# Split operands for two more experts' second products, and the first two gated experts run by halves

## The reference, cut to what matters

```python
logits = tokens @ router_w.T
topv, topi = jax.lax.top_k(logits, K)                 # K = 2 of E = 8
w = jax.nn.softmax(topv, axis=-1)
gate = zeros((T, n_experts)).at[arange(T)[:, None], topi].add(w)
for e in range(n_experts):
    h = gelu(tokens @ w1[e].T)                        # 128 -> 256
    y = h @ w2[e].T                                   # 256 -> 128
    out = out + gate[:, e:e + 1] * y
```

## Time and profile before

| | |
|---|---|
| median of 3 runs | 139.96 us (139.6 to 140.53) |
| the profiled execution, its own time | 139.31 us |
| its span, first to last instruction | 137.6 us |
| mean granted TensorE clock | 0.937 |
| busy: TensorE, VectorE, ScalarE, GpSimd | 83%, 83%, 60%, 28% |

### The profile page before, as it was taken

One profiled execution on the slowest core, in us unless ns is written; L12 is line 12 of the kernel. 1 busy time (PEld: TensorE's weight loads), 2 busy tenths in 40 slices (PEclk: granted clock), 3 DMA queues, 4 the chain that ended last, 5 costly groups with the idle time before them and its releaser, 6 DMA issues.

```text
span 137.6 us, 1963 instructions
## 1 busy us (share of the span) xinstructions
PE 113.8 (83%) x598; PEld 82.6 (60%) x598; DVE 113.6 (83%) x324; ACT 82.4 (60%) x157; POOL 38.3 (28%) x59
## 2 busy tenths in 40 slices
PE   6999999999999999999999998885999200068990
PEld 4686768477565788877664877763768100045670
DVE  5898985998419999999947897889698899799872
ACT  3542495825756658787436124177978999860730
POOL 1018302230359910069301284422021011100000
PEclk9999999999999999999999999999999955555999
DMA  4995000000159722222000000000000000000004
GB/s 122 369 412 231 0 0 0 0 0 22 64 156 341 261 74 91 75 78 76 0 5 0 0 0 2 5 0 2 0 0 0 0 2 0 0 0 0 5 0 152
DMA packets 4413, 8.76 MB, mean 64 GB/s; under 512 B 417, under 2 KB 1825, under 8 KB 4146
## 3 DMA queue, kind: packets, MB, share of 16 engines
q1 hardware_dynamic: 4400, 8.62, 17.8%
q10 hardware_dynamic: 2, 0.00, 0.0%
HBM read 8.07 MB, written 0.56 MB: 63 GB/s over the span
## 4 chain that ended last, share of the span: by engine, by line
PE 59%; DVE 20%; issue 9%; ACT 5%; POOL 4%; DVEq 0%; POOLq 0%
PE bank L1441 7%; PE bank L1392 6%; PE bank L1387 6%; PE bank L1389 5%; PE bank L1421 5%; PE bank L1269 4%; PE bank L1295 3%; PE bank L1290 3%; PE bank L1289 3%; DVE amax_p L1164 3%; POOL q_soft L487 2%; PE bank L1624 2%; DVE amax_g L1155 2%; PE bank L1275 2%; DVE hidden L1200 2%
## 5 line engine op out<-in xcount | busy, mean ns | idle before, releaser
L1269 PE MATMUL bank<-zero 128*128 128x256 f16 x112 | 18.7, 321 | 15.7 <-ACT ng L706 14.0
L567 ACT ACTIVATE hidden<-bank 128x512 f32<-128x512 f32 x32 | 18.6, 593 | 12.4 <-PE bank L1392 11.2
L1269 PEld LDWEIGHTS bank<-zero 128*128 128x128 f16 x112 | 12.4, 114 | 19.6 <-ACT ng L706 14.5
L1387 PE MATMUL bank<-xhi,we_hi 128*128 128x512 f32 x32 | 17.2, 538 | 0.0
L993 DVE TENSOR_TENSOR hidden<-hidden,q_exp 128x512 f32<-128x512 f32 x12 | 10.2, 873 | 4.7 <-DMA q_exp<-gates 2.9
L414 POOL TENSOR_TENSOR rstd<-var,neg_half 128x4 f32<-128x4 f32 x7 | 7.1, 1014 | 20.0 <-DVE var L758 20.0
L1392 PE MATMUL bank<-xlo,we_hi 128*128 128x512 f32 x32 | 12.7, 406 | 0.0
L1389 PE MATMUL bank<-xhi,we_lo 128*128 128x512 f32 x32 | 12.6, 394 | 0.0
L1441 PE MATMUL bank<-hidden,wexp 128*128 128x512 f32 x24 | 11.9, 592 | 0.0
L427 POOL TENSOR_TENSOR we_lo<-wexp,we_hi 128x256 fp32r<-128x256 f32 (+1 forms) x8 | 7.9, 1006 | 12.8 <-DVE gate L928 10.0
L573 ACT ACTIVATE high_parts<-hidden 128x512 fp32r<-128x512 f32 x12 | 7.6, 634 | 4.3 <-DVE hidden L993 4.2
(11 more groups left out here) (272 smaller groups left out, 297.3 us busy)
## 6 DMA issues: line engine op xcount, KB each, us to landing
wexp<-in_experts SPq DMA_DIRECT2D x2, 1024.0 KB, 7.8
q_exp<-gates SPq DMA_DIRECT2D x6, 256.0 KB, 3.1
q_soft<-gates SPq DMA_DIRECT2D x6, 256.0 KB, 3.4
wq<-in_lpbq SPq DMA_DIRECT2D x1, 576.0 KB, 9.7
stream<-in_x SPq DMA_DIRECT2D x2, 256.0 KB, 3.7
xn<-gates SPq DMA_DIRECT2D x1, 512.0 KB, 5.9
x<-gates SPq DMA_DIRECT2D x1, 512.0 KB, 6.7
pa<-in_packa SPq DMA_DIRECT2D x1, 325.0 KB, 3.0
```

Of the source, the lines that this page charges most:

```text
L567: act.activation(ge[p % NB][:, :], bank[4 + p % NB][:, :], ACT.Gelu).then_inc(gelu_done, 1)
L1269: mm(bank[b][:, 0:256], zero16[:, 0:128], zero16[:, 0:256], start=True, stop=True)
L1387: mm(out_, w_hi[e][:, k], half(xhi, h), start=True, stop=False)
```

## The change

Experts 2 and 6 leave `NATIVE`, so that experts 2 to 6 are split and only expert 7 of the gated ones is native. Units 8 to 15 (experts 2 and 3) are now ordered by halves: both chunks of expert 2 and of expert 3 for half 0, then the same for half 1. Units 24 to 31 were ordered in this way before. SyncE's queue asks for the rows of experts 2 and 3 for a half as soon as that half's gates are out. VectorE's `weight_values` stands ahead of the first `gate_unit` instead of at p = 11, and at p = 11 `low` comes ahead of the next `gate_unit`. ScalarE's and TensorE's lists are written as before, and `high`, `high_weights` and `y_unit` in them follow `split`.

```diff
-        NATIVE = (0, 1, 2, EXPERTS - 2, EXPERTS - 1)
+        NATIVE = (0, 1, EXPERTS - 1)
         LAST = UNITS - 2 * FIRST
-        ORDER = [0, 1, 4, 5, 2, 3] + list(range(6, LAST))
-        ORDER += [LAST + e * FIRST + h * FC + c for h in range(HALVES) for e in range(2) for c in range(FC)]
+
+        def by_halves(first):
+            return [first + e * FIRST + h * FC + c for h in range(HALVES) for e in range(2) for c in range(FC)]
+
+        ORDER = by_halves(0) + by_halves(GATED) + list(range(2 * GATED, LAST)) + by_halves(LAST)
...
                 sp.wait_ge(gates_out[h], 16)
-                e = PAIRS[h][0]
-                sp.dma_start(rows_at(h), half(gates, h)[e:e + 1, :].broadcast_to([128, HT])).then_inc(rows_in[h], 16)
-            for k in range(HALVES, len(PAIRS)):
+                for k in range(LATE * h, LATE * h + LATE):
+                    e = PAIRS[k][0]
+                    sp.dma_start(rows_at(k), half(gates, h)[e:e + 1, :].broadcast_to([128, HT]))\
+                        .then_inc(rows_in[k], 16)
+            for late in range(LATE):
+                sp.dma_start(late_rows[late], gates[late:late + 1, :].broadcast_to([128, TOKENS]))\
+                    .then_inc(late_in[late], 16)
+            for k in range(RING, len(PAIRS)):
                 e, h = PAIRS[k]
-                if k >= RING:
-                    sp.wait_ge(gated, (k - RING + 1) * FC)
+                sp.wait_ge(gated, (k - RING + 1) * FC)
                 sp.dma_start(rows_at(k), half(gates, h)[e:e + 1, :].broadcast_to([128, HT]))\
                     .then_inc(rows_in[k % RING], 16)
-                if k == RING - 1:
-                    for late in range(LATE):
-                        sp.dma_start(late_rows[late], gates[late:late + 1, :].broadcast_to([128, TOKENS]))\
-                            .then_inc(late_in[late], 16)
...
+            weight_values()
             gate_unit(GATED)
             for p in range(GATED, UNITS):
+                if p == GATED + FIRST - 1:
+                    low(p)
                 if p + 1 < UNITS:
                     gate_unit(p + 1)
-                if split(UNIT[p][0]):
+                if split(UNIT[p][0]) and p != GATED + FIRST - 1:
                     low(p)
-                if p == 11:
-                    weight_values()
-                elif p in (13, 14):
+                if p in (13, 14):
                     late_gate(1, p - 13)
```

## The result

The changed kernel takes 143.65 us (143.25 to 143.94, 4 runs) against 139.94: a ratio of 1.0265, with an interval of 1.0233 to 1.0296. It is slower by 3.7 us where 1.8 were forecast, above the stated range. The profiled execution took 143.43 us, with a span of 141.7.

The account below looks back on a forecast made before the run. PE was taken to set the pace: 2.27 us wait at unit 8, plus 0.4 and 0.4 for late low parts, minus 1.28 of removed work, gives 1.8 us more, 139.96 to 141.8 us; range 140.8 to 143.3.

Parts of the forecast that it names:

- its removed work: Eight units of experts 2 and 6 become split, each 0.16 us cheaper on PE: 1.28 us less.
- The wait at unit 8: PE waits for ScalarE's high parts, queued behind an activation and two weight conversions: 2.27 us lost.
- The edits around the split: Wider weights, earlier rows, swapped order and moved residual products: costed at nothing.
- the high parts would not be there in time: Against a rival at unit 8: high parts ready in time, 138.7 us with no stall; chance 0.04.
- PE's idle time from 39 to 76 us: Sign: the prediction is wrong if this is less than 2.3 us or more than 4.2.
- its signs of being wrong: PE idle time outside 2.3 to 4.2 us, or a clock leaving 2.4 GHz, from 39 to 76 us.
- a rival with a chance of 0.05: Clock falls after the stall at unit 8: 2.7 us on top, 144.5 us; chance 0.05.
- "I take 0.4 us" at unit 8: Unit 8's third pass waits for VectorE's low part: 0.4 us, from 0.26 to 0.5.
- "I take 0.4 us" at units 24 and 25: PE waits for low parts that meet GpSimd's last-layer weights: 0.4 us, from nothing to 1.1.
- I called it a bound: Two low parts at units 24 and 25, stretched by 0.75 us each, make PE wait up to 1.1 us.
- The rival of the lock: VectorE loses to GpSimd at every meeting in units 8 to 11 and 23 to 29: 3.1 us more, 143.1; chance 0.12.
- A cost taken as nothing: Expert 2's wider low weights on GpSimd lie ahead of a 6.49 us pause: nothing, or 0.3 us if uncovered.

Follow-up runs that it names:

- e15: e2 with GpSimd's low parts of the last layer's weights moved behind the last gating; ratio 0.997 to the kernel before.
- e1: The changed kernel with experts 2 and 6 native again, the new order, rows and moved weight values kept; ratio 0.9985 to the kernel before.
- e13: The changed kernel with expert 2 alone split and expert 6 native; 143.67 us against 140.11 for the kernel before.
- e7: The kernel before, with TensorE made to wait ahead of unit 8 for GpSimd's low weights of all experts, nothing split; 144.06 us against 139.61.
- e3: The changed kernel with 18 zero products filling TensorE's wait ahead of unit 8; 142.85 us against 139.82 for the kernel before.
- e2: The changed kernel with expert 6 alone split and expert 2 native; 139.13 us against 139.82 for the kernel before.
- e14: The changed kernel with ScalarE's conversions before unit 10's activation, first products six units ahead, GpSimd's last-layer columns behind the last gating; ratio 1.0038 to the kernel before.
- e7b: The kernel before, with TensorE made to wait ahead of unit 8 until ScalarE has converted all experts' weights, nothing split; ratio 1.0114.
- e4: The changed kernel with ScalarE's conversions for experts 6 and 7 moved behind unit 9's high parts; 143.0 us against 139.82 for the kernel before.
- e9: The changed kernel with ScalarE's conversions for experts 6 and 7 moved ahead of unit 10's activation; ratio 1.0126 to the kernel before.

## Why the prediction was wrong

**What held.** PE sets the pace, and its removed work is what the change can win: the stage of e15 is 0.81 us shorter, 0.64 for four cheaper products and the 0.17 that e1 is rid of (PE's two short waits of the earlier trace rows, which the prediction left out when it said that PE had no idle time to give back). The wait at unit 8 was worked out at 2.27 us from ScalarE's list and measured 2.29. The edits around the split cost nothing that shows (e1). That the high parts would not be there in time was right. PE's idle time from 39 to 76 us came to 2.5 us, between the 2.3 and 4.2 that the prediction allowed; of its signs of being wrong, the one that showed was the clock. (VectorE isn't nearly full throughout slices 12 to 22, as the prediction reads the earlier trace rows: it is at 1 in slice 12 and at 4 and 7 in 21 and 22. Nothing in the sum rests on that.)

**The step that failed** is the sum, 2.27 + 0.4 + 0.4 - 1.28, which has no term for the clock. That stood beside it as a rival with a chance of 0.05. In the changed kernel's trace the terms of the sum came out near their size: 2.29 for the wait, 0.55 for unit 8's low part, 0.37 for unit 25's. What was missing is the work at 1.2 GHz, some 1.5 us: the turns of units 8 and 9 took 2.19 us more, of which the sum had 0.4. By the trace, 2.29 + 2.19 + 0.37 - 1.28 - 0.17 = 3.4 us, the 3.38 of the stage (the 0.17 are the two short waits, gone here as in e1). The rival's chance came from a row in which PE idled for 2.5 us at 2.4 GHz. That row only tells that the clock was still up by then; the next, at 110.2, was at a half, and nothing in the trace had PE idle for 2 to 2.5 us and then keep its clock. In the changed kernel and in e13 the clock fell after waits of 2.29 and 2.06 us, 1.0 and 1.4 us after PE had resumed. By itself such a fall costs 1.4 to 1.6 us (e7), where the rival had 2.7.

**Near by luck: the waits for low parts.** "I take 0.4 us" at unit 8 and "I take 0.4 us" at units 24 and 25 came near only with the clock down and PE late. With the clock up they measured 0.91 and 1.12 us (e3), and the sum is 2.29 + 0.91 + 1.12 - 1.28 = 3.0, the 2.98 of e3's stage. So the clock costs 1.5 us where it falls, and taking it out wins 0.4 (3.38 against 2.98). With the clock held the time was 142.85 us (e3), inside the stated range, but 3.0 us above the kernel before where 1.8 were forecast. At units 8 and 9 the stretched operations are two in a row, and I priced one. At units 24 and 25 I took the middle because GpSimd gets in only where DVE pauses; but VectorE does pause there, at 66.3 us for 0.22 us in e3, and once GpSimd has got in, operations come out stretched in turn. The earlier trace rows had this, 1.38 us and then 1.50; I called it a bound and didn't let it stand. The rival of the lock came near this time, with a chance of 0.12 (its upper ends add up to 2.9 us, not the 3.1 it gave).

**How the rivals were put together.** The lock and the clock were priced as alternatives to the forecast. Here both came, the clock in the changed kernel and the lock as soon as the clock is held, and each hides part of the other. The range ended at the lock alone.

**A cost taken as nothing:** from unit 8's first pass to unit 11's it takes 4.92 us in the changed kernel (34.71 to 39.63) and 4.77 before (34.12 to 38.89), 0.15 us more. It is 4.92 in e13 and 4.77 and 4.76 in e1 and e2, so it comes with the split of expert 2. That it is expert 2's wider low weights, which delay VectorE's gates of the second half, is argued from the place; no run takes it out.

**Left open:** whether splitting expert 2 can pay at all. In e14 the stage only comes out even: PE still waits 0.26, 0.36, 0.25 and 0.34 us for the low parts of units 8, 9, 28 and 29, nearly all of the 1.28 that it saves. No place was tried for the columns that costs nothing elsewhere.

## What to carry to other kernels

Where an engine at the bound is made cheaper, look for the next bound first: before splitting work over three engines, see how far the other two are from being late, place by place, and add up all waits that arise, as they can come on top of each other. A sum from a full engine's rows holds only while its clock does: where a change opens a wait, price the work behind it at the lower clock too. Work that stands ahead in a queue's list (here two weight conversions) is a wait for whoever needs the instruction behind it, and moving it moves its followers on other engines. In this kernel the split pays where its consumer isn't the first of its queue: expert 6 alone gives 0.3%, expert 2 alone costs 2.5%.

## What the runs showed of the hardware

TensorE's clock can fall after PE has resumed work. In the changed kernel PE waited from 40.3 to 42.6, and the clock went to 1.2 GHz at 43.6 and back to 2.4 at 47.0. In e13 it was at 1.2 GHz from 43.8 to 47.1, with PE at work since 42.4. In e7 it was there from 42.8 to 46.1, and PE resumed at 43.06. PE had waited 2.29, 2.06 and 3.08 us in these. In the kernels in which it waited 1.46 us (e7b, e4, e9) the clock stayed at 2.4 GHz, as it did when the wait of 2.29 us was filled with products of zeros (e3).

A VectorE operation with two SBUF inputs that meets one of GpSimd with SBUF inputs took 1.04 to 1.78 us in the rows above instead of 0.68, while GpSimd's operation, kept out by VectorE working back to back, took 4.53 us, and 1.28 in the changed kernel (at 70.35, above). The Trainium skill (SBUF — State Buffer, section "SBUF: two separate sides") says of such a pair that the one that starts first holds the shared ports for its whole instruction and the other is blocked. The traces agree: in e3 a gating that starts at 69.47, while GpSimd is at work from 68.97 to 70.42, takes 1.50 us and ends at 70.97, 0.55 us after GpSimd's, little less than it takes alone.
